# Attention weighting: ScalarE also weighs the last two steps of each batch's last quarter, VectorE's operation there covers two steps

## The chip, the core and the metric

The kernel runs on one core of a Trainium2 chip. The metric is device time in microseconds (us) of one execution, the median of several runs. The engines are TensorE (PE in the profile, PEld for its weight loads), VectorE (DVE), ScalarE (ACT), GpSimd (POOL) and SyncE (SP); each works through its own instructions in order, and they wait for one another by semaphores.

## What is computed

A two-layer graph network over 3125 nodes and 53125 edges (25000 pairs in both directions and one loop a node), all in float32. Each layer adds a message-passing step, a mixer and a mixture of experts to the nodes' features. The change concerns only the message passing of the first layer, attention over the edges into a node, with 8 heads of 32 columns:

```
q = (x @ Wq + bq).reshape(n, H, C)
k = (x @ Wk + bk).reshape(n, H, C)
v = (x @ Wv + bv).reshape(n, H, C)
alpha = jnp.einsum('ehc,ehc->eh', q[dst], k[src]) / jnp.sqrt(jnp.float32(C))
amax = jax.ops.segment_max(alpha, dst, num_segments=n)
ex = jnp.exp(alpha - amax[dst])
denom = jax.ops.segment_sum(ex, dst, num_segments=n)
attn = ex / denom[dst]
msg = (v[src] * attn[:, :, None]).reshape(-1, H * C)
out = jax.ops.segment_sum(msg, dst, num_segments=n)
```

The kernel multiplies v[src] by ex (this is the weighting), sums the weighted rows and ex itself by node, and divides once a node later.

## The kernel before

The edges are sorted by their target and cut into 440 steps of up to 128 edges that belong to one block of 128 nodes. Four steps are a half (`hh`; the prediction calls its place in a batch half 0 to 3, and the title a quarter), two steps are a duo or pair (`p`), and 16 steps are a batch (`j`): 27 full batches and one of 8 steps. `at_kv` holds 32 steps, each with a K part (256 columns), a V part (256) and 8 columns for ex.

What each engine does in `attention`, lines 887 to 1260, in its own fixed order:

- GpSimd (line 949) gathers K and V rows of each step's edges, one indirect DMA a step. A gather waits until TensorE has summed the step 32 before it.
- TensorE `fetch(dd)` (line 1041): for a pair of steps, spreads q from nodes to edges, 6 matmuls (the profile shows two fetches in a row as one row of 12). `attend(j, x)` (lines 1052 and 1066): for pair x of a batch, one matmul that clears and then the matmuls that sum the weighted V rows and ex by node. Their stationary operand is the edge one-hot.
- ScalarE `edge_hot(hh)` (lines 988 and 993): builds the edge one-hot of one half, four Abs and one Relu of the four together. Line 1014 is the exponential of each half, four in a batch. `weigh` (line 1003) multiplies V by ex for half 2: for each of 4 steps and 8 heads one Copy of 32 columns with a scale.
- VectorE `multiply` (1138) multiplies K by q, `reduce` (1147) sums over a head, `weight` (1156) multiplies V by ex for halves 0, 1 and 3, 1024 columns an operation, `add` (1167) adds a pair's sums to `acc`. Between them stands the maximum by segments: scans (1231, 1232, 1239, 1240, 1248, 1249) over scores that TensorE has transposed (line 1088).

Scores and maximum of batch j are made while batch j - 1 is attended. In TensorE's order a cycle is: `fetch` of two pairs, pair 0, a fetch, pairs 1 to 3, a fetch, pairs 4 and 5, a fetch (`at + 8`), pairs 6 and 7, two fetches (`at + 9`, `at + 10`), the transpose of the new scores. In VectorE's: the weighting of half 0 and 1, of half 3 (behind `add` of pair 3), `add` of pairs 4 and 5, the last reductions, `add` of 6 and 7, and then the scans, at whose end line 1255 makes what ScalarE's exponential of the next batch reads.

Pairs 4 and 5 belong to half 2, pairs 6 and 7 to half 3. A pair's matmuls wait for the edge one-hot of their half (`built`) and for its weighting (`weighted`, counted by VectorE's operations, or `weighed`, by ScalarE's steps). Here "one-hot 2" is that of half 2 of the batch being attended, made by `edge_hot(4 * j + 2)`.

Of the kernel before, what the change touches and what calls it, by code (L numbers as in the profile page):

```python
# [14 lines left out]
P = 128  # L15
N = 3125
D = 256
# [14 lines left out]
H1 = 8  # L32
# [67 lines left out]
def wide(ap, shape):  # L100
    return ap.to_broadcast(shape)
# [779 lines left out]
Q4 = U // 2  # L881
# [5 lines left out]
def attention(nc, k, e, q_parts, kv_tab, acc):  # L887
# [3 lines left out]
    HD = D // H1  # L891
# [5 lines left out]
    with Scope(nc) as s:  # L897
        kv = s.sb("at_kv", [P, RING * Q4, 2 * D + H1])
# [34 lines left out]
        weighed = s.sem("at_weighed")  # L933

        def slot(hh):
            return slice(hh % RING * Q4, hh % RING * Q4 + Q4)

        def halves_of(j):
            return list(range(4 * j, min(4 * j + 4, halves))) if 0 <= j < batches else []

        with nc.Block(no_gpsimd_drain=True) as block:
            @block.gpsimd
            def _(pool):
                for t in range(T1):
                    if t >= RING * Q4:
                        pool.wait_ge(summed, t - RING * Q4 + 1)
                    if t >= AHEAD + 2:
                        pool.wait_ge(multiplied, (t - AHEAD) // 2)
                    nc.gpsimd.indirect_dma_start(  # L949
                        out=kv[:, t % (RING * Q4), 0:2 * D], out_offset=None, in_=kv_tab,  # L950
                        in_offset=bass.IndirectOffsetOnAxis(ap=e.src[:, t:t + 1], axis=0)).then_inc(got[t // Q4 % RING], 16)
# [25 lines left out]
            @block.scalar  # L977
            def _(act):
                a = nc.scalar.activation
                made = [0]  # L980

                def edge_hot(hh):
                    if hh >= halves:
                        return
                    if hh:
                        act.wait_ge(built, hh)
                    for u in range(Q4):
                        a(away_e[:, u, :], k.count_row[:, 0:P], ACT.Abs, bias=e.rel[:, hh * Q4 + u:hh * Q4 + u + 1], scale=-1.0).then_inc(away, 1)
                    made[0] += Q4
                    act.wait_ge(away, made[0])  # L990
                    if hh >= NEDGE:
                        act.wait_ge(summed, (hh - NEDGE + 1) * Q4)
                    a(hot_e[:, hh % NEDGE], away_e[:, :, :], ACT.Relu, bias=k.ones[:, 0:1], scale=-1.0).then_inc(built, 1)  # L993

                def weigh(j, us):
                    hh = 4 * j + 2
                    if hh >= halves:
                        return
                    act.wait_ge(exped, hh + 1)
                    for u in us:  # L1000
                        for h in range(H1):
                            row = kv[:, hh % RING * Q4 + u, D + h * HD:D + (h + 1) * HD]
                            ins = a(row, row, ACT.Copy, scale=kv[:, hh % RING * Q4 + u, 2 * D + h:2 * D + h + 1])  # L1003
                        ins.then_inc(weighed, 1)

                edge_hot(0)
                for j in range(batches):
                    if j:
                        act.wait_ge(fell, j)
                        a(fade[:, j % 2:j % 2 + 1], fall[:, j % 2:j % 2 + 1], ACT.Exp, scale=SCALE).then_inc(faded, 1)  # L1010
                    act.wait_ge(diffed, j + 1)
                    for x, hh in enumerate(halves_of(j)):
                        act.wait_ge(got[hh % RING], 16 * Q4 * (hh // RING + 1))
                        a(kv[:, slot(hh), 2 * D:W + D], below[:, x * Q4:(x + 1) * Q4, :], ACT.Exp, scale=SCALE).then_inc(exped, 1)
                    edge_hot(4 * j + 1)
                    weigh(j, (0, 1))
                    weigh(j, (2, 3))
                    edge_hot(4 * j + 2)
                    edge_hot(4 * j + 3)
                    edge_hot(4 * j + 4)  # L1020

            @block.tensor
            def _(pe):
# [21 lines left out]
                def attend(j, *xs):  # L1045
                    for x in xs:
                        p = j * U + x
                        if j < 0 or p >= duos:
                            continue
                        if p >= 2:  # L1050
                            pe.wait_ge(added, p - 1)
                        nc.tensor.matmul(ps_a[p % 2][:, 1, 0:W], nothing[:, 0:P], nothing[:, :], start=True, stop=False, skip_group_check=True)
                        pe.wait_ge(built, p // 2 + 1)
                        if p // 2 % 4 == 2:
                            pe.wait_ge(weighed, Q4 * (p // 8 + 1))
                        else:
                            pe.wait_ge(weighted, p // 8 * 3 + (0, 1, 0, 2)[p // 2 % 4] + 1)
                        for u in range(2):
                            t = 2 * p + u
                            if u == 0:  # L1060
                                to = ps_a[p % 2][:, 0, 0:W]
                            else:
                                r = nc.s_assert_within(where[p // Q4][U + p % Q4], 0, 1,
                                                       skip_runtime_bounds_check_because="a step's block is its neighbour's or the next one")
                                to = ps_a[p % 2][:, ds(r, 1), 0:W].rearrange("p a w -> p (a w)")
                            nc.tensor.matmul(to, hot_e[:, t // Q4 % NEDGE, t % Q4, :], kv[:, t % (RING * Q4), D:2 * D + H1],  # L1066
                                             start=(u == 0), stop=(u == 1), skip_group_check=True).then_inc(summed, 1)
                        if p % Q4 == Q4 - 1:
                            del where[p // Q4]
                for x in range(4):  # L1070
                    fetch(x)
                for j in range(batches + 1):
                    at, i = U * j, j - 1
                    fetch(at + 4)
                    fetch(at + 5)
                    attend(i, 0)
                    fetch(at + 6)
                    attend(i, 1, 2, 3)
                    fetch(at + 7)
                    attend(i, 4, 5)  # L1080
                    fetch(at + 8)
                    attend(i, 6, 7)
# [22 lines left out]
            def _(dve):  # L1105
                v = nc.vector
# [43 lines left out]
                def weight(A, x):  # L1150
                    if x >= len(A):
                        return
                    hh = A[x]
                    dve.wait_ge(exped, hh + 1)
                    rows = kv[:, slot(hh), D:2 * D].rearrange("p u (h d) -> p u h d", d=HD)
                    v.tensor_tensor(rows, rows, wide(kv[:, slot(hh), 2 * D:2 * D + H1].unsqueeze(3), [P, Q4, H1, HD]),
                                    ALU.mult).then_inc(weighted, 1)

                def add(j, x):
# [33 lines left out]
                for j in range(batches + 1):  # L1193
                    S, A, i, at = halves_of(j), halves_of(j - 1), j - 1, U * j
                    last = j == batches
                    h, x = j % 2, score[:, j % 2]
                    load(2 * i)
                    multiply(at + 3)
                    rescale(i)
                    weight(A, 0)  # L1200
                    reduce(S, 0)
                    weight(A, 1)
                    if 1 <= i < batches:
                        dve.wait_ge(rescaled, i)
# [7 lines left out]
                    add(i, 3)  # L1212
                    multiply(at + 5)
                    weight(A, 3)
                    add(i, 4)
                    reduce(S, 2)
# [2141 lines left out]
```

## Time and profile before

| | us |
|---|---|
| median of 3 runs | 3025.67 |
| the runs | 3021.57 to 3026.47 |
| the profiled execution | 3023.47 |
| its span | 3021.7 |
| VectorE busy in the span | 2035.0 (67%) |
| TensorE busy | 2281.1 (75%) |
| GpSimd busy | 1641.5 (54%) |
| ScalarE busy | 1375.9 (46%) |

The profiled execution is one run of the program with every instruction recorded; all durations and places below come from it. Its span starts at 0 with the first instruction. The attention lies between about 284 and 1003 us. "Granted clock" is the share of TensorE's full clock (1.00 is 2.4 GHz, 0.50 is 1.2 GHz). A matmul's end is modelled.

### The profile page before, as it was taken

The page shows a single profiled execution, that of the slowest core. Times are in us where ns is not written, and L with a number is a line of the kernel's source. Part 1 is how long each engine was busy: PE and PEld are TensorE (multiplying, and loading weights), DVE is VectorE, ACT ScalarE, POOL GpSimd, SP SyncE. Part 2 cuts the span into 40 slices and gives each one's busy share as a digit, 9 for nine tenths or more (in the row PEclk, how much of TensorE's full clock was granted, in tenths as well). Part 3 has the DMA queues.
Part 4 walks back from the last instruction along what each step waited for, and adds up shares of the span by engine and source line. Part 5 has one row for each costly group of instructions (what it writes and reads, how often), then busy time and mean ns, then how long its engine had stood idle before and what let it go on. Part 6 is the DMA issues. An engine that isn't in the chain of part 4 may idle for free. (4 is left out here: it accounts for less than half of the span.)

```text
span 3021.7 us, 41600 instructions
## 1 busy us (share of the span) xinstructions
PE 2281.1 (75%) x11076; PEld 1512.9 (50%) x11076; DVE 2035.0 (67%) x4208; ACT 1375.9 (46%) x4369; POOL 1641.5 (54%) x1754
## 2 busy tenths in 40 slices
PE   3997777777777656699965578777778788888785
PEld 2554455555555455556623223222337677777664
DVE  4564899999999888701075699999984722222586
ACT  0221566666666244321242588888972122222232
POOL 1544766666664204567776677777752077777200
PEclk8998788888888855599976799999989689989898
DMA  3212766666664022233232233333321211111004
GB/s 105 54 41 80 217 192 197 195 193 193 195 193 140 1 58 73 58 88 94 87 85 62 82 105 105 103 104 105 105 63 16 61 37 36 32 37 37 17 1 182
DMA packets 165629, 289.12 MB, mean 96 GB/s; under 512 B 55933, under 2 KB 99970, under 8 KB 165407
## 3 DMA queue, kind: packets, MB, share of 16 engines
q0 software_dynamic: 79344, 187.14, 22.8%
q1 hardware_dynamic: 73906, 80.60, 8.6%
q10 hardware_dynamic: 12156, 18.72, 1.7%
q8 instruction: 102, 1.67, 0.2%
q14 instruction: 121, 0.98, 0.1%
HBM read 250.08 MB, written 36.25 MB: 95 GB/s over the span
## 5 line engine op out<-in xcount | busy, mean ns | idle before, releaser
L949 POOL DMA_INDIRECT at_kv<-kv_tab,e_src x440 | 431.9, 981 | 265.5 <-PE at_a L1066 152.4
L2358 PE MATMUL cv_ps<-cv_msg,cv_hot 128*128 128x512 f32 x880 | 431.1, 632 | 145.3 <-DVE acc L2413 126.5
L2345 POOL DMA_INDIRECT cv_x<-x_tab,e_src x440 | 423.7, 963 | 147.7 <-issue 98.8
L2794 POOL DMA_INDIRECT gs_h<-h_tab,fc_q x312 | 295.1, 946 | 184.9 <-issue 93.6
L2358 PEld LDWEIGHTS cv_ps<-cv_msg,cv_hot 128*128 128x128 f32 x880 | 162.0, 198 | 414.1 <-ACT cv_msg L2371 252.6
L2009 POOL DMA_INDIRECT pairs<-gating_pair,gating_place x281 | 275.9, 982 | 149.0 <-issue 66.5
L2371 ACT ACTIVATE cv_msg<-cv_x,factors 128x64 f32<-128x64 f32 x1320 | 356.5, 333 | 0.0
L2413 DVE TENSOR_TENSOR acc<-acc,cv_ps 128x256 f32 x880 | 306.9, 412 | 6.5 <-PE cv_ps L2358 3.8
L2369 ACT ACTIVATE cv_msg<-cv_x,factors 128x256 f32<-128x256 f32 x440 | 217.8, 495 | 122.6 <-DMA cv_x<-x_tab,e_src 122.6
L1066 PE MATMUL at_a<-at_kv,at_hot_e 128*128 128x264 f32 x880 | 252.9, 416 | 13.9 <-ACT at_hot_e L993 9.9
L1041 PE MATMUL at_q<-q_parts,at_hot_n 128*128 x1320 | 228.2, 329 | 42.5 <-DVE at_hot_n L1128 21.1
L2751 ACT ACTIVATE gs_x_hid<-gs_x_h,x_b 128x128 f32<-128x128 f32 x320 | 91.5, 369 | 303.9 <-PE gs_x_h L2718 303.9
L2728 PE MATMUL gs_x_y<-x_w,gs_x_hid 128*128 128x256 f32 x640 | 171.6, 419 | 51.6 <-DVE gs_y L2758 51.5
L1041 PEld LDWEIGHTS at_q<-q_parts,at_hot_n 128*128 128x128 bf16 x1320 | 147.3, 113 | 112.7 <-issue 61.2
L1066 PEld LDWEIGHTS at_a<-at_kv,at_hot_e 128*128 128x128 f32 x880 | 163.7, 207 | 47.3 <-ACT at_hot_e L993 19.0
L1003 ACT ACTIVATE at_kv<-at_kv 128x32 f32<-128x32 f32 x864 | 185.6, 306 | 0.0
L1167 DVE TENSOR_TENSOR acc<-acc,at_a 128x528 f32 x220 | 154.0, 700 | 39.5 <-PE at_a L1066 31.9
L2871 DVE TENSOR_REDUCE gs_as_dst<-gs_d 128x32 f32<-128x96 f32 x39 | 10.1, 258 | 250.7 <-DMA gs_h<-h_tab,fc_q 250.7
L2728 PEld LDWEIGHTS gs_x_y<-x_w,gs_x_hid 128*128 128x128 f32 x640 | 128.7, 210 | 73.7 <-issue 46.9
L2718 PE MATMUL gs_x_h<-xnT,x_w 128*128 128x128 f32 x1280 | 161.0, 283 | 0.0
L2718 PEld LDWEIGHTS gs_x_h<-xnT,x_w 128*128 128x128 f32 x1280 | 157.9, 199 | 2.7
L1138 DVE TENSOR_TENSOR at_kv<-at_kv,at_q 128x512 f32<-128x512 f32 x220 | 147.2, 680 | 15.9 <-DVE at_ends L1240 6.1
(546 smaller groups left out, 4437.9 us busy)
## 6 DMA issues: line engine op xcount, KB each, us to landing
x_space<-in_L_ffn_w SPq DMA_DIRECT2D x16, 1024.0 KB, 7.0
at_rel_row<-e_rel_rows SPq DMA_DIRECT2D x55, 256.0 KB, 4.5
experts_out<-gs_y ACTq DMA_DIRECT2D x20, 512.0 KB, 2.7
x_y<-experts_out SPq DMA_DIRECT2D x20, 512.0 KB, 6.9
at_kv<-kv_tab,e_src POOLq DMA_INDIRECT x440, 3.7
cv_x<-x_tab,e_src POOLq DMA_INDIRECT x440, 2.8
kv_tab<-p_qkv SPq DMA_DIRECT2D x25, 256.0 KB, 2.0
gs_h<-h_tab,fc_q POOLq DMA_INDIRECT x312, 2.4
```

The lines of the kernel that those rows point to most:

```text
L949: nc.gpsimd.indirect_dma_start(out=kv[:, t % (RING * Q4), 0:2 * D], out_offset=None, in_=kv_tab, in_offset=bass.IndirectOffsetOnAxis(ap=e. ...
L1041: ins = nc.tensor.matmul(ps_q[dd % 3][:, u, :], hot_n[:, t // Q4 % NHOT, t % Q4 * P:(t % Q4 + 1) * P], q_parts[:, ds(b, 1), n, :].rearrang ...
L1066: nc.tensor.matmul(to, hot_e[:, t // Q4 % NEDGE, t % Q4, :], kv[:, t % (RING * Q4), D:2 * D + H1], start=(u == 0), stop=(u == 1), skip_gro ...
L2009: nc.gpsimd.indirect_dma_start(out=pairs, out_offset=bass.IndirectOffsetOnAxis(ap=place_i[:, c:c + 1], axis=0), in_=pair[:, c, :], in_offs ...
L2345: nc.gpsimd.indirect_dma_start(out=xg[:, i % RT, u, :], out_offset=None, in_=x_tab, in_offset=bass.IndirectOffsetOnAxis(ap=e.src[:, t:t + ...
L2358: nc.tensor.matmul(ps[u % R][:, :], hot[:, i % 2, u, :], msg[:, i % 2, u, :], start=True, stop=True).then_inc(summed, 1)
L2369: nc.scalar.activation(msg[:, h, u, 0:D], xg[:, i % RT, u, :], ACT.Copy, scale=factor[:, t:t + 1, 0])
L2371: ins = nc.scalar.activation(msg[:, h, u, D + m * M:D + (m + 1) * M], xg[:, i % RT, u, 0:M], ACT.Copy, scale=factor[:, t:t + 1, 1 + m])
L2413: v.tensor_tensor(row, row, ps[u % R][:, n * D:(n + 1) * D], ALU.add).then_inc(added, 1)
L2718: ins = self.nc.tensor.matmul(self.ps_h[e % 2][:, f * P:(f + 1) * P], self.x1.w1[:, e, c, f * P:(f + 1) * P], self.xnT[:, c, b * P:(b + 1) ...
L2728: ins = self.nc.tensor.matmul(self.ps_y[e % 2][:, 0:D], self.hid[:, e % 2, f, :], self.x1.w2[:, e, f, :], start=(f == 0), stop=(f == FX // ...
L2794: nc.gpsimd.indirect_dma_start(out=hg[:, i % RT, u, :], out_offset=None, in_=h_tab, in_offset=bass.IndirectOffsetOnAxis(ap=e.src[:, i * U ...
```

## The change

`weigh` gets the half as an argument. Besides half 2 of each batch, ScalarE weighs the last two steps of half 3, 16 more Copy instructions, placed behind one-hot 2 and ahead of one-hot 3. VectorE's operation for half 3 covers only its first two steps. Pair 6 still waits for VectorE's count and pair 7 now for ScalarE's, which grows by 6 steps a batch where it grew by 4.

```diff
-                def weigh(j, us):
-                    hh = 4 * j + 2
+                def weigh(j, x, us):
+                    hh = 4 * j + x
...
                     edge_hot(4 * j + 1)
-                    weigh(j, (0, 1))
-                    weigh(j, (2, 3))
+                    weigh(j, 2, (0, 1))
+                    weigh(j, 2, (2, 3))
                     edge_hot(4 * j + 2)
+                    weigh(j, 3, (2, 3))
                     edge_hot(4 * j + 3)
                     edge_hot(4 * j + 4)
...
                         if p // 2 % 4 == 2:
-                            pe.wait_ge(weighed, Q4 * (p // 8 + 1))
+                            pe.wait_ge(weighed, 6 * (p // 8) + Q4)
+                        elif p % 8 == 7:
+                            pe.wait_ge(weighed, 6 * (p // 8) + 6)
                         else:
                             pe.wait_ge(weighted, p // 8 * 3 + (0, 1, 0, 2)[p // 2 % 4] + 1)
...
-                    rows = kv[:, slot(hh), D:2 * D].rearrange("p u (h d) -> p u h d", d=HD)
-                    v.tensor_tensor(rows, rows, wide(kv[:, slot(hh), 2 * D:2 * D + H1].unsqueeze(3), [P, Q4, H1, HD]),
+                    n = Q4 if x < 3 else 2
+                    mine = slice(slot(hh).start, slot(hh).start + n)
+                    rows = kv[:, mine, D:2 * D].rearrange("p u (h d) -> p u h d", d=HD)
+                    v.tensor_tensor(rows, rows, wide(kv[:, mine, 2 * D:2 * D + H1].unsqueeze(3), [P, n, H1, HD]),
                                     ALU.mult).then_inc(weighted, 1)
```

ScalarE's order in one batch before, from the exponentials (L1014) on; L988 and L993 are an edge one-hot, L1003 the weighting:

```order
L1014 ACTIVATE at_kv<-at_below 128x4x8 x4
L988 ACTIVATE at_away_e<-count_row,e_rel 128x128 x4
L993 ACTIVATE at_hot_e<-at_away_e,ones 128x512
L1003 ACTIVATE at_kv<-at_kv 128x32 x32
L988 ACTIVATE at_away_e<-count_row,e_rel 128x128 x4
L993 ACTIVATE at_hot_e<-at_away_e,ones 128x512
L988 ACTIVATE at_away_e<-count_row,e_rel 128x128 x4
L993 ACTIVATE at_hot_e<-at_away_e,ones 128x512
L988 ACTIVATE at_away_e<-count_row,e_rel 128x128 x4
L993 ACTIVATE at_hot_e<-at_away_e,ones 128x512
```

And now, at the same place:

```order
L1014 ACTIVATE at_kv<-at_below 128x4x8 x4
L988 ACTIVATE at_away_e<-count_row,e_rel 128x128 x4
L993 ACTIVATE at_hot_e<-at_away_e,ones 128x512
L1003 ACTIVATE at_kv<-at_kv 128x32 x32
L988 ACTIVATE at_away_e<-count_row,e_rel 128x128 x4
L993 ACTIVATE at_hot_e<-at_away_e,ones 128x512
L1003 ACTIVATE at_kv<-at_kv 128x32 x16
L988 ACTIVATE at_away_e<-count_row,e_rel 128x128 x4
L993 ACTIVATE at_hot_e<-at_away_e,ones 128x512
L988 ACTIVATE at_away_e<-count_row,e_rel 128x128 x4
L993 ACTIVATE at_hot_e<-at_away_e,ones 128x512
```

The one-hots of half 3 and of the next batch's half 0 moved behind 16 copies. (Line numbers of ScalarE's rows stay; VectorE's weighting is line 1156 before and 1161 after.)

VectorE's order around the weighting of half 3 before:

```order
330 L1138 TENSOR_TENSOR at_kv<-at_kv,at_q 128x2x256
331 L1128 TENSOR_SCALAR at_hot_n<-at_rel_row,count_col 128x512
332 L1156 TENSOR_TENSOR at_kv<-at_kv 128x4x256
333 L1167 ISA
334 L1167 TENSOR_TENSOR acc<-acc,at_a 128x528
```

And now:

```order
330 L1141 TENSOR_TENSOR at_kv<-at_kv,at_q 128x2x256
331 L1131 TENSOR_SCALAR at_hot_n<-at_rel_row,count_col 128x512
332 L1161 TENSOR_TENSOR at_kv<-at_kv 128x2x256
333 L1172 ISA
334 L1172 TENSOR_TENSOR acc<-acc,at_a 128x528
```

Nothing moved here; the operation covers 2 steps of 256 columns instead of 4. TensorE's order is the same before and after.

## Rows read from the trace of the kernel before

**Rows 1.** The page's first line:

```profile
span 3021.7 us, 41600 instructions
```

**Rows 2.** Windows: length, busy time (x instructions) of PE, PEld, DVE, ACT, POOL; clock; DMA:

```profile
300.00:1000.00 700.00, 521.78 (x2601) 360.84 (x2601) 636.65 (x1227) 416.72 (x1546) 419.29 (x427) 0.82 0.63 186
```

**Rows 3.** Waits from 300 to 1000 us: total, times, longest:

```profile
PEld at_a L1066 <- ACT at_hot_e L993: 19.0, 18, 2.5
...
DVE at_runs L1231 <- PE at_t L1088: 0.9, 1, 0.9
```

**Rows 4.** Groups by line, 300 to 1000 us: busy us, mean ns of one:

```profile
L1003 ACT ACTIVATE at_kv<-at_kv 128x32 f32<-128x32 f32 x864 | 185.6, 306 | 0.0
...
L1138 DVE TENSOR_TENSOR at_kv<-at_kv,at_q 128x512 f32<-128x512 f32 x216 | 144.6, 680 | 11.7 <-DVE at_ends L1240 6.1 <-DMA at_kv<-kv_tab,e_src 2.8 <-issue 0.9
...
L1156 DVE TENSOR_TENSOR at_kv<-at_kv 128x1024 f32<-128x1024 f32 x83 | 100.9, 1217 | 0.0
```

**Rows 5.** Timeline of ScalarE: start, length of the merged row [idle before it]:

```profile
317.14 0.59 ACT L1014 ACTIVATE at_kv<-at_below 128x32 f32<-128x32 f32 x4 [24.87 <-DVE at_below L1255]
...
643.53 0.59 ACT L1014 ACTIVATE at_kv<-at_below 128x32 f32<-128x32 f32 x4 [0.59 <-DVE at_below L1255]
...
645.32 0.72 ACT L993 ACTIVATE at_hot_e<-at_away_e,ones 128x512 f32<-128x512 f32 x1
645.95 6.87 ACT L1003 ACTIVATE at_kv<-at_kv 128x32 f32<-128x32 f32 x32
652.73 1.26 ACT L988 ACTIVATE at_away_e<-count_row,e_rel 128x128 f32<-128x128 f32 x4
654.02 0.72 ACT L993 ACTIVATE at_hot_e<-at_away_e,ones 128x512 f32<-128x512 f32 x1
...
656.09 0.72 ACT L993 ACTIVATE at_hot_e<-at_away_e,ones 128x512 f32<-128x512 f32 x1
...
668.57 0.59 ACT L1014 ACTIVATE at_kv<-at_below 128x32 f32<-128x32 f32 x4 [0.59 <-DVE at_below L1255]
...
970.29 0.59 ACT L1014 ACTIVATE at_kv<-at_below 128x32 f32<-128x32 f32 x4 [0.59 <-DVE at_below L1255]
```

**Rows 6.** Timeline of TensorE, pair 4 to the transpose of the scores:

```profile
654.79 1.16 PE L1066 MATMUL at_a<-at_kv,at_hot_e 128*128 128x264 f32 x4 [0.25 <-ACT at_hot_e L993]
...
655.90 1.05 PE L1066 MATMUL at_a<-at_kv,at_hot_e 128*128 128x264 f32 x4
...
657.56 1.05 PE L1066 MATMUL at_a<-at_kv,at_hot_e 128*128 128x264 f32 x4
...
658.72 1.10 PE L1066 MATMUL at_a<-at_kv,at_hot_e 128*128 128x264 f32 x4
659.66 1.49 PE L1041 MATMUL at_q<-q_parts,at_hot_n 128*128 x12
661.57 0.33 PE L1088 MATMUL at_t<-ident,at_score 128*128 128x128 f32 x1 [0.42 <-DVE at_score L1225]
```

**Rows 7.** Timeline of VectorE, the add of pair 7 and the first scan:

```profile
662.34 0.70 DVE L1167 TENSOR_TENSOR acc<-acc,at_a 128x528 f32 x1 [0.21 <-DVE acc L1167]
662.96 0.41 DVE L1231 TENSOR_TENSOR_SCAN at_runs<-at_flags,at_t 128x128 f32<-128x128 f32 x1
```

**Rows 8.** Timeline in the last full batch: its pair 4, its first scan:

```profile
981.55 1.16 PE L1066 MATMUL at_a<-at_kv,at_hot_e 128*128 128x264 f32 x4 [2.17 <-ACT at_hot_e L993]
...
986.96 0.41 DVE L1231 TENSOR_TENSOR_SCAN at_runs<-at_flags,at_t 128x128 f32<-128x128 f32 x1
```

**Rows 9.** Timeline of TensorE early in the next cycle, fetches and pair 0:

```profile
669.80 2.74 PE L1041 MATMUL at_q<-q_parts,at_hot_n 128*128 x12 [0.52 <-DVE at_hot_n L1128]
...
672.55 1.97 PE L1066 MATMUL at_a<-at_kv,at_hot_e 128*128 128x264 f32 x4
```

**Rows 10.** Windows as in rows 2: an early stretch of a cycle, and an empty one:

```profile
669.80:674.50 4.70, 4.70 (x18) 3.35 (x19) 3.95 (x5) 4.67 (x20) 0.59 (x1) 0.50 0.52 172
979.40:981.50 2.10, 0.00 (x0) 0.00 (x0) 1.84 (x2) 2.06 (x6) 0.00 (x0) 1.00 0.00 0
```

## The prediction

> **What bounds the kernel now.** The profiled execution has a span of 3021.7 us [rows 1], 3023.47 us with what lies around it; the median of the three timed runs is 3025.67 us. Only the attention is touched, so I read that stage alone, engine by engine: from 300 to 1000 us VectorE is busy 636.65 of 700 us, TensorE 521.78, ScalarE 416.72, GpSimd 419.29 [rows 2]. By the shares VectorE is the bound and ScalarE has 40% of the stage free, which is what the change spends. Shares are means over a cycle, though, so next come the waits and then one cycle.
>
> The waits: VectorE almost never waits for the transposed scores (once, 0.9 us), while the weight loads of line 1066 already wait 18 times for ScalarE's edge one-hot [rows 3]. So ScalarE, idle as it is on the average, is late at one place of the cycle.
>
> The cycle: 26 of the 28 batches take 25.12 us on the mean, (970.29 - 317.14)/26 between the starts of line 1014 [rows 5]. I count from such a start; in the sample batch it is 643.53, and the next is 668.57. In this cycle batch j's steps are attended. ScalarE's copies (half 2) run from 645.95 to 652.73, one-hot 2 is ready at 654.02 + 0.72 = 654.74 (+11.21), one-hot 3 at 656.09 + 0.72 = 656.81 (+13.28) [rows 5]. TensorE starts pair 4 at 654.79, 0.05 behind one-hot 2, having waited 0.25; pair 6 at 657.56 (+14.03), pair 7 at 658.72, the two fetches at 659.66, the transpose of the scores at 661.57 [rows 6]. VectorE adds pair 7 at 662.34 and starts the first scan at 662.96 [rows 7]. Over the 26 batches that scan stands on the mean 19.57 us behind the cycle's start, and 5.55 us before the next one (26 pairs of a row of line 1014 and one of line 1231, of which 643.53, 662.96 and 668.57 stand in the rows [rows 5, 7]). A cycle is thus: from the start to the scan, and the serial scans behind it.
>
> **The change part by part.** *VectorE's part removed.* Line 1156 takes 1.217 us for 1024 elements; no row has the same form with 512, the nearest is line 1138, 512 elements, 0.680 us [rows 4]. Half of 1.217 would be 0.61. I take 0.68, the row of the same size: 0.54 us saved in each of 27 batches, 14.5 us if VectorE alone set the cycle.
>
> *ScalarE's part added.* Two steps of eight heads are 16 copies in each of 27 batches, 432 in all. One lasts 306 ns, but 32 of them begin and end within 645.95 to 652.73, so 0.212 us each [rows 4, 5]; 16 take 3.39 us, 91.5 us over the stage. Their amount fits into ScalarE's idle time, but not their place: they stand between one-hots 2 and 3. Copies begin 0.63 us behind the start of the one-hot before them (645.32 to 645.95), and the next one-hot is ready 2.01 us behind their end (652.73 to 654.74) [rows 5]. So one-hot 3 is ready at 654.02 + 0.63 + 3.39 + 2.01 = 660.05, +16.52 instead of +13.28. Its user, pair 6, stands at +14.03 now: 0.75 us of slack against 3.24 us of delay.
>
> *What queues behind that wait.* TensorE works in order. Behind pair 6 stand pair 7, the two fetches and the transpose. Pair 6 starts at +16.57. Pair 7 is 1.11 behind it (654.79 to 655.90), the fetches 0.94 behind that (658.72 to 659.66), and their 12 matmuls last 1.49 us at full clock; the next matmul may start 0.05 before a group's modelled end (654.79 + 1.16 against 655.90) [rows 6]. The transpose then starts at 16.57 + 1.11 + 0.94 + 1.49 - 0.05 = +20.06, lasts 0.33, and the scan follows 0.05 later (the gap seen from one-hot to matmul): +20.44.
>
> *VectorE at that time.* It reaches add 6 half a microsecond earlier than now, waits for pair 6, and can start add 7 when pair 7 is done, 16.57 + 1.11 + 1.05 = +18.73, about +18.8. The scan is 0.62 behind add 7 (662.34 to 662.96) [rows 7], so at +19.4 it would be free; it waits one more microsecond for the transpose. The 0.54 us saved stand before these waits and are lost in them whole. What is late next is the transpose, a wait that is hardly there now.
>
> *The new waits themselves.* TensorE's wait of pair 7 on the copies costs nothing: they end at 654.02 + 0.63 + 3.39 = +14.5, before one-hot 3. One-hot 4, pushed to about +18.6, is needed by the first pair of the next cycle, beyond +25. GpSimd's gathers are released by pairs 6 and 7 about 2.5 us later; it is busy 419.29 of 700 us [rows 2], a share that a longer cycle lowers further, so I take it as hidden.
>
> *The sum.* In 26 batches the scan moves from +19.57 to +20.44, and the 5.55 us behind it stay: 26 x 0.87 = 22.6 us. The last full batch has no fetches and no next scores, so it gets the delay nearly undiluted: pair 6 at 970.29 + 16.57 = 986.86, pair 7 at 987.97, done at 989.02, add 7 at 989.07, scan at 989.69 instead of 986.96 [rows 8]: 2.7 us. Together 25.3 us, which is 3048.8 on the profiled execution's 3023.47 and **3051 us** on the median. In this case alone, with the start of the transpose uncertain by 0.25 us a batch, the time lies between 3043 and 3058.
>
> The Trainium skill, "ScalarE: Activation LUTs", section "Rules for kernel authors", sends multiplications to VectorE and not to ScalarE. Here that rule would also have the change lose, by engine time: 3.39 us of ScalarE bought with 0.54 us of VectorE. The sum does not rest on it.
>
> **The rivals.** *The clock falls in the new hole.* TensorE now has nothing between about +14.2 and +16.57. At the lower clock (0.5 granted, 1.2 GHz, from 669.80 to 674.50 [rows 10]) 12 fetch matmuls take 2.74 us and a pair 1.97, against 1.49 and 1.05 [rows 9, 6]. For two pairs and the fetches this is 0.92 + 0.92 + 1.25 = 3.1 us at most, all on the path. That stretch lies behind the sparse one around the transpose, so a cycle does lose the clock where it is sparse. Against it speak two rows: before the last full batch's pair 4 TensorE waited 2.17 us, and the grant stayed at 1.00 (2.4 GHz) through the empty stretch, the pair lasting 1.16 us [rows 8, 10]. If it falls in a third of the batches, 9 x 2.7 = 24 us more: 3075. In all of them: 3124. [...]
>
> *The delay is hidden.* If TensorE had the transpose out before VectorE wants it, the scan would stand at +19.4, 0.17 us earlier than now: 26 x -0.17 + 2.7 = -2 us, 3024, no change. It decides whether 12 matmuls lie between pair 7 and the transpose; by the program they do.
>
> *VectorE stays the bound (the change does what the shares promise).* Then 27 x 0.54 = 14.5 us are gained: 3011. This needs one-hot 3 ready by +14.1, that is 16 copies in 0.8 us instead of 3.39. The rows of the 864 copies leave no room for it [rows 4].
>
> **How the numbers follow.** Forecast (one-hot 3 late, clock held) 0.64: 3051. Clock falls in part of the batches 0.24: 3075 and beyond. Hidden 0.07: 3024. VectorE's gain 0.05: 3011. The range of 8 in 10 takes the forecast's own and the clock's up to a third of the batches: 3040 to 3076. About 0.2% (6 us) is what a measurement can tell: faster 0.05, same 0.07, slower 0.88.
>
> **What would show it.** In the profile after: TensorE's wait for the edge one-hot, 19.0 us of weight loads now, grows by some 27 x 2.3 = 60 us; a wait of VectorE's scan for the transpose appears, about 1 us in each of 26 batches; the starts of the exponentials stand about 26.0 apart; the 2-step operation lasts 0.68 us; ScalarE's copies number 1296. Wrong: pair 6 starting before +16, the scan before +20, the 2-step operation with no wait behind it, or matmuls of pairs 6 and 7 near 2 us (the clock).

## The result and the profile after

| | us |
|---|---|
| before, median of 6 runs | 3025.35 (3020.24 to 3026.47) |
| changed, median of 6 runs | 3086.26 (3083.67 to 3088.01) |
| ratio, with its 95% interval | 1.0205 (1.0192 to 1.0218) |
| the changed kernel's profiled span | 3081.3 |

The change costs 61 us, where 25 were forecast and 51 was the end of the range. The direction and the place were right, the size was not. Busy time does not explain it, as the page's first part and the window over the attention (with columns as in [rows 2]) show:

```profile
span 3081.3 us, 42031 instructions
...
PE 2317.4 (75%) x11075; PEld 1546.4 (50%) x11076; DVE 2023.6 (66%) x4208; ACT 1464.4 (48%) x4801; POOL 1629.8 (53%) x1754
```

```profile
300.00:1052.00 752.00, 548.06 (x2578) 383.75 (x2578) 618.82 (x1217) 503.09 (x1971) 406.01 (x426) 0.79 0.59 173
```

In the whole span VectorE works 11 us less, ScalarE 88 us and TensorE 36 us more, all of them with time to spare, and the stage is 62 us longer: from the first batch's exponentials to the last one's it was 991.59 - 317.14 = 674.45 us and is 1052.52 - 315.90 = 736.62. The waits from 300 to 1060 us, with columns as in [rows 3]:

```profile
DVE acc L1172 <- PE at_a L1069: 90.8, 136, 3.8
PEld at_a L1069 <- ACT at_hot_e L993: 78.8, 32, 3.2
...
DVE at_runs L1236 <- PE at_t L1091: 22.4, 27, 1.6
```

The weight loads' wait for the one-hot went from 19.0 to 78.8 us, and a wait of the first scan for the transpose appeared, 22.4 us against 0.9 [rows 3]. One cycle shows how. ScalarE, in the cycle that starts at 644.83:

```profile
644.83 0.59 ACT L1014 ACTIVATE at_kv<-at_below 128x32 f32<-128x32 f32 x4 [0.59 <-DVE at_below L1260]
...
655.33 0.72 ACT L993 ACTIVATE at_hot_e<-at_away_e,ones 128x512 f32<-128x512 f32 x1
655.96 3.49 ACT L1003 ACTIVATE at_kv<-at_kv 128x32 f32<-128x32 f32 x16
...
660.64 0.72 ACT L993 ACTIVATE at_hot_e<-at_away_e,ones 128x512 f32<-128x512 f32 x1
```

One-hot 3 is ready at 661.36, +16.53; the prediction had +16.52. TensorE, from pair 6 to the transpose, which answers to [rows 6]:

```profile
661.42 2.13 PE L1069 MATMUL at_a<-at_kv,at_hot_e 128*128 128x264 f32 x4 [2.39 <-ACT at_hot_e L993]
...
663.56 1.56 PE L1069 MATMUL at_a<-at_kv,at_hot_e 128*128 128x264 f32 x4
664.96 1.47 PE L1042 MATMUL at_q<-q_parts,at_hot_n 128*128 x12
666.27 0.27 PE L1091 MATMUL at_t<-ident,at_score 128*128 128x128 f32 x1
```

Pair 6 starts at +16.59 and lasts 2.13 us, pair 7 1.56; in the cycle below that kept its clock they take 1.16 and 1.05. The windows say why: the grant falls from 1.00 to 0.50 (2.4 to 1.2 GHz) at the end of the empty stretch.

```profile
658.80:661.30 2.50, 0.23 (x3) 0.00 (x0) 2.50 (x7) 2.47 (x9) 1.89 (x2) 0.97 0.70 213
661.60:664.60 3.00, 3.00 (x8) 2.20 (x9) 1.88 (x3) 1.80 (x5) 2.39 (x3) 0.50 0.76 221
```

By windows of 0.4 us over the stage, this happens between +16.3 and +17.9 in 26 of the 27 cycles: from the last tenths of the hole to 1.3 us behind its end, when pair 6 or 7 is running. Pair 6's wait is 1.95 to 2.39 us in the first 26 cycles and 2.96 in the last. The one cycle that held its clock, through a wait of 2.15 us, is a control within the profile; its pair 6, fetches and transpose:

```profile
743.34 1.16 PE L1069 MATMUL at_a<-at_kv,at_hot_e 128*128 128x264 f32 x4 [2.15 <-ACT at_hot_e L993]
...
744.44 1.05 PE L1069 MATMUL at_a<-at_kv,at_hot_e 128*128 128x264 f32 x4
745.33 1.47 PE L1042 MATMUL at_q<-q_parts,at_hot_n 128*128 x12
746.64 0.27 PE L1091 MATMUL at_t<-ident,at_score 128*128 128x128 f32 x1
```

It took 25.76 us, the others of the first 26 27.40 us on the mean. VectorE in the cycle from 644.83 waits for pair 6, for pair 7 and for the transpose, one after the other:

```profile
663.69 0.70 DVE L1172 TENSOR_TENSOR acc<-acc,at_a 128x528 f32 x1 [0.88 <-PE at_a L1069]
665.27 0.70 DVE L1172 TENSOR_TENSOR acc<-acc,at_a 128x528 f32 x1 [0.87 <-PE at_a L1069]
666.65 0.42 DVE L1236 TENSOR_TENSOR_SCAN at_runs<-at_flags,at_t 128x128 f32<-128x128 f32 x1 [0.68 <-PE at_t L1091]
```

### The profile page after: what moved, and what is told of

Read it like the earlier page. It is cut to its first block and busy times, and to the rows that moved or that the text cites. A ratio compares the mean times of both kernels' runs of the same rounds, so it can differ in the third digit from the quotient of the medians.

```text
span 3081.3 us, 42031 instructions
## 1 busy us (share of the span) xinstructions
PE 2317.4 (75%) x11075; PEld 1546.4 (50%) x11076; DVE 2023.6 (66%) x4208; ACT 1464.4 (48%) x4801; POOL 1629.8 (53%) x1754
## 5 line engine op out<-in xcount | busy, mean ns | idle before, releaser
L949 POOL DMA_INDIRECT at_kv<-kv_tab,e_src x440 | 419.4, 953 | 331.4 <-PE at_a L1069 191.9
L1069 PE MATMUL at_a<-at_kv,at_hot_e 128*128 128x264 f32 x880 | 297.6, 475 | 69.9 <-ACT at_hot_e L993 66.0
L1003 ACT ACTIVATE at_kv<-at_kv 128x32 f32<-128x32 f32 x1296 | 279.7, 306 | 0.0
L1069 PEld LDWEIGHTS at_a<-at_kv,at_hot_e 128*128 128x128 f32 x880 | 187.8, 236 | 121.5 <-ACT at_hot_e L993 78.8
L1141 DVE TENSOR_TENSOR at_kv<-at_kv,at_q 128x512 f32<-128x512 f32 x220 | 147.4, 681 | 12.7 <-DVE at_ends L1245 6.2
```

The source lines that it names most:

```text
L949: nc.gpsimd.indirect_dma_start(out=kv[:, t % (RING * Q4), 0:2 * D], out_offset=None, in_=kv_tab, in_offset=bass.IndirectOffsetOnAxis(ap=e. ...
```

## The experiments

All were timed in turn with the kernel before on the same chip; its medians there were 3026.6, 3023.3 and 3024.5 us for the three groups of runs. Where two medians differ by a few microseconds I also give the stage, from the first batch's exponentials to the last one's, in the two profiles: two profiles of one kernel agree there to 0.2 us (653.81 and 653.62, the run with one-hots built ahead and its repetition), while what lies behind the stage takes 2027 to 2035 us in the 13 profiles, without a tie to the edit.

### Is it the clock, or the late one-hot itself?

**The hole filled.** In the changed kernel's `attend`, behind the clearing matmul:

```diff
+                        for _ in range(18 if x == 6 else 0):
+                            nc.tensor.matmul(ps_a[p % 2][:, 1, 0:W], nothing[:, 0:P], nothing[:, :], start=True, stop=False, skip_group_check=True)
```

> The changed kernel with 18 more clearing matmuls (zeros, bfloat16, the same as the one that is there) on TensorE ahead of pair 6's wait, in the hole of 2.4 us. It computes the same. Theory (the clock falls in the hole): with the hole filled the granted clock stays at 1.00 until behind the transpose, pairs 6 and 7 last 1.16 and 1.05 us again, the cycle is 25.8 us as in the one batch that held its clock, and the time is 3086.3 - 26 x 1.6 = about 3045 us, although TensorE does more. Rival (ScalarE's copies into at_kv slow TensorE's or VectorE's access to the same memory, and the clock only goes along with it): pairs stay near 2 us and the time at 3083 or above.

3041.1 us, 1.0049 of before (1.0031 to 1.0066). TensorE in the same place now:

```profile
667.79 2.19 PE L1055 MATMUL at_a<-at_nothing 128*128 128x264 bf16 x18
670.22 1.16 PE L1071 MATMUL at_a<-at_kv,at_hot_e 128*128 128x264 f32 x4 [0.24 <-ACT at_hot_e L993]
```

No cycle loses its clock there, the mean of the first 26 is 25.78 us, and 45 of the 61 us are gone, by 486 matmuls more on zeros and nothing else. What stays, 14.5 us on the medians and 694.31 - 674.45 = 19.9 us between the exponentials of the two profiles, is the delay alone. The copies' access to the memory is not the cause of these 45 us: they are all still there.

**The delay alone.** In the kernel before, between one-hots 2 and 3:

```diff
                     edge_hot(4 * j + 2)
...
+                        for n in range(16):
+                            ins = a(idle[:, n, :], k.count_row[:, 0:HD], ACT.Copy, scale=k.ones[:, 0:1]).then_inc(idled, 1)
                     edge_hot(4 * j + 3)
```

> The kernel before, VectorE's operations as they were, with 16 copies of 32 columns into a scratch tile between one-hots 2 and 3: the delay alone, with nothing weighed by it. Theory (one-hot 3's delay and the hole are all that matters, VectorE's 0.54 us saved are lost in its waits): the time is that of the changed kernel, 3083 to 3090 us. Rival (the copies' access to at_kv): no such access here, so cycles near 25.8 to 26.0 and 3045 us. If VectorE's saving had counted after all, 3086 + 14.5 = 3101.

3088.0 us, 1.0200 (1.0183 to 1.0217): the whole loss, although ScalarE weighs no more than before and VectorE's operations have their full size. Pair 6 of one cycle:

```profile
663.13 2.13 PE L1074 MATMUL at_a<-at_kv,at_hot_e 128*128 128x264 f32 x4 [2.53 <-ACT at_hot_e L995]
```

Its one-hot 3 is 0.14 us later than the changed kernel's. The clock falls in 25 of the 27 cycles; the two that keep it do so through waits of 2.34 and 2.53 us. So what VectorE saves is worth next to nothing here, not 14.5 us.

### How long may the hole be?

**Nine matmuls instead of 18**, which leaves pair 6 a wait of 0.9 to 1.4 us (1.9 in the last full batch).

> As the run with 18 clearing matmuls ahead of pair 6's wait, with 9: the hole on TensorE shrinks from 2.4 to about 1.4 us and is not closed. It computes the same. Theory (the length of the hole decides whether the clock falls in it): 1.4 us is less than the 2.17 us that one pair of before waited through at full clock, so the clock holds in nearly all batches: 3041 to 3048 us. Rival (any hole in this place drops it): 3080 us or more; a mixture of cycles of 25.8 and 27.3 us would put it between.

3043.0 us, 1.0066 (1.0049 to 1.0083), as with the hole closed. The clock falls in none of the 27. One of them:

```profile
669.24 1.16 PE L1071 MATMUL at_a<-at_kv,at_hot_e 128*128 128x264 f32 x4 [1.24 <-ACT at_hot_e L993]
```

**Four**, which leaves 1.4 to 1.9 us (2.5 in the last full batch).

> The changed kernel with 4 clearing matmuls more ahead of pair 6's wait: a hole of about 1.9 us, between the 1.4 us that held the clock in the run with 9 and the 2.4 us of the changed kernel that lost it in 26 of 27 batches. It computes the same. If the hole's length decides with an edge below 1.9 us: cycles of 27.3 us and 3080 or more. If the edge lies above: 25.8 and 3043. If it depends on where in the cycle the hole falls as well: both kinds of cycle in one run, between 3043 and 3086.

3056.4 us, 1.0110 (1.0089 to 1.0130): both kinds of cycle in one run. In the profile 5 of 27 lose the clock, the other cycles take 25.8. Pairs 6 and 7 of a cycle that lost it and of one that held it, the hole alike:

```profile
544.05 1.19 PE L1071 MATMUL at_a<-at_kv,at_hot_e 128*128 128x264 f32 x4 [1.93 <-ACT at_hot_e L993]
545.25 1.97 PE L1071 MATMUL at_a<-at_kv,at_hot_e 128*128 128x264 f32 x4
...
597.24 1.16 PE L1071 MATMUL at_a<-at_kv,at_hot_e 128*128 128x264 f32 x4 [1.93 <-ACT at_hot_e L993]
598.35 1.05 PE L1071 MATMUL at_a<-at_kv,at_hot_e 128*128 128x264 f32 x4
```

So length is not all. In the five that fell the hole was 1.9 us and the clock had risen at +3.9 to +4.3 of the same cycle; in those that held it rose at +4.4 or later, up to +7.9. All five fell at +17.6 to +17.9, 1.0 to 1.3 us behind the hole's end. The hole of 1.4 us never lost it here, that of 1.9 us sometimes, that of 2 us and more nearly always (51 of the 54 cycles of the changed kernel and of the run with the delay alone). That the place of the hole against the clock's earlier rise counts as well is what the five and the 22 suggest; no run moved the one without the other.

### Smaller versions of the edit

**One-hot 3 ahead of the copies.**

```diff
                     edge_hot(4 * j + 2)
-                    weigh(j, 3, (2, 3))
                     edge_hot(4 * j + 3)
+                    weigh(j, 3, (2, 3))
                     edge_hot(4 * j + 4)
```

> The changed kernel with one-hot 3 ahead of the 16 added copies and not behind them. It computes the same. One-hot 3 is ready at +13.3 as in the kernel before, pair 6 starts on time at +14.0, and pair 7 waits for the copies until about +16.8, a hole of 1.6 us between the pairs. Theory: pair 7 stands 0.9 us earlier than in the changed kernel, the transpose at +19.0, the scan at +19.4, about where it is in the kernel before, and the clock holds in the shorter hole: 3020 to 3030 us. If the clock falls here too, in all batches: about 3065. Rival (the order of the two doesn't matter, the copies' 3.39 us do): 3080 and above.

3025.5 us, 1.0006 (0.9996 to 1.0015): no loss, and no gain. Pair 7 now waits, 1.0 to 1.5 us, and the clock holds in each of the first 26 cycles. In the cycle that starts at 641.93:

```profile
658.75 1.13 PE L1069 MATMUL at_a<-at_kv,at_hot_e 128*128 128x264 f32 x4 [1.46 <-ACT at_kv L1003]
659.72 1.47 PE L1042 MATMUL at_q<-q_parts,at_hot_n 128*128 x12
661.03 0.27 PE L1091 MATMUL at_t<-ident,at_score 128*128 128x128 f32 x1
```

Two lines in another order take back all 61 us. The same instructions run.

**One step instead of two** (8 copies; VectorE's operation over three steps).

> The changed kernel with half of the edit: ScalarE weighs only the last step of half 3 (8 copies, 1.7 us), VectorE's operation covers three steps (768 elements, about 0.95 us). It computes the same. Theory: one-hot 3 is ready at about +14.9, pair 6 waits 0.7 us, the clock holds, the transpose could start at +18.3 and the scan is VectorE's: it waits for pair 7, done at about +17.1, less than now. So the cycle keeps its length or loses up to 0.27 us: 3018 to 3027 us. Rival (each copy between the one-hots costs its time): half of the loss, about 3055.

3023.5 us, 1.0000 (0.9990 to 1.0010). One-hot 3 is ready at +14.84. Pair 6 waits 0.4 to 0.7 us and keeps its full clock, as in this cycle:

```profile
657.68 1.16 PE L1070 MATMUL at_a<-at_kv,at_hot_e 128*128 128x264 f32 x4 [0.44 <-ACT at_hot_e L993]
```

The transpose stands at +18.2, 1.7 us earlier than in the cycle of the changed kernel that held its clock, and VectorE does not wait for it. The loss is not proportional to the copies: half of them cost nothing.

### What is VectorE's half microsecond worth?

**VectorE's part alone**, in the kernel before: its operation for half 3 covers two steps and nobody weighs the other two.

```diff
+                    n = Q4 if x < 3 else 2
+                    mine = slice(slot(hh).start, slot(hh).start + n)
```

> The kernel before with VectorE's operation for half 3 over two steps and nothing in its place: the last two steps of each full batch's half 3 stay unweighted. ScalarE's and TensorE's instructions are those of before. It prices VectorE's 0.54 us a batch by themselves. Theory (VectorE sets the cycle in the stretch from that operation to the scans once one-hot 3 is on time): 3026 - 14.5 = about 3012 us. Rival (VectorE's time there is slack, and the cycle hangs on pair 4's wait for one-hot 2 at +11.2 and TensorE behind it): no change, 3020 to 3027.

3022.8 us, 1.0006 (0.9996 to 1.0015): nothing; the stage is 674.45 - 673.21 = 1.2 us shorter. Here my theory fell, and the rival with pair 4 stands. VectorE before, in the cycle that starts at 643.53:

```profile
654.84 1.20 DVE L1156 TENSOR_TENSOR at_kv<-at_kv 128x1024 f32<-128x1024 f32 x1
656.10 0.70 DVE L1167 TENSOR_TENSOR acc<-acc,at_a 128x528 f32 x1
```

And in this run, in the cycle that starts at 643.32:

```profile
654.62 0.67 DVE L1158 TENSOR_TENSOR at_kv<-at_kv 128x512 f32<-128x512 f32 x1
655.89 0.70 DVE L1169 TENSOR_TENSOR acc<-acc,at_a 128x528 f32 x1 [0.59 <-PE at_a L1066]
...
662.93 0.41 DVE L1233 TENSOR_TENSOR_SCAN at_runs<-at_flags,at_t 128x128 f32<-128x128 f32 x1
```

The operation is 0.53 us shorter, and the next one, the add of pair 4, waits 0.59 us: it starts at +12.57 in both. Pair 4 starts only when ScalarE's one-hot 2 is ready, at +11.2, change or no change. So it is in 16 of the first 26 cycles; in the other ten pair 4 starts later, at +11.3 to +11.9, behind TensorE's own earlier work. The add of pair 4 waits for TensorE in all 26, and did in 10 before. VectorE is busy 91% of the stage [rows 2] and not what this stretch hangs on.

### ScalarE's order mended

**The one-hots ahead of time**, in the kernel before: those of halves 1 and 2 are built at the end of the cycle before, where ScalarE waits some 9 us.

```diff
                 edge_hot(0)
+                edge_hot(1)
+                edge_hot(2)
...
-                    edge_hot(4 * j + 1)
                     weigh(j, (0, 1))
                     weigh(j, (2, 3))
-                    edge_hot(4 * j + 2)
                     edge_hot(4 * j + 3)
                     edge_hot(4 * j + 4)
+                    edge_hot(4 * j + 5)
+                    edge_hot(4 * j + 6)
```

> The kernel before with the same earlier one-hots and nothing else: what the new order gives alone. Theory: pair 4's waits for one-hot 2 (19.0 us in all, 0.25 to 0.8 us a batch) go, most of it hidden behind VectorE: 3018 to 3026 us. The difference to the changed kernel in the same order is VectorE's 0.54 us in 27 batches, 14.5 us.

3010.0 us, 0.9952 (0.9936 to 0.9967). The gain, 16.5 us on the medians and 674.45 - 664.14 = 10.3 us in the stage, is more than I had expected at most: pair 4's wait was not hidden behind VectorE, the cycle hung on it. Pair 4 now never waits for one-hot 2 in the first 26 cycles, and its add never for pair 4. (The one-hot of half 1 moved too; what each of the two gives was not tried.)

**The same order with the change in it**, `weigh(j, 3, (2, 3))` behind `weigh(j, 2, ...)`.

> The changed kernel with ScalarE's one-hots built ahead: one-hots 1 and 2 of the next batch are built at the end of a cycle, where ScalarE is idle, and behind the exponentials come the weighting of half 2, that of half 3 and only then one-hot 3. It computes the same. Theory (place, not amount, was wrong): one-hot 3 is ready near +12.9, pair 6 doesn't wait, VectorE is the bound and its 0.54 us show: 3011 us, down to 3005 where pair 4's wait goes too. Rival (432 more copies cost by themselves): above 3025.

3006.9 us, 0.9927 (0.9910 to 0.9944). ScalarE does all 48 copies in a row, and one-hot 3 is ready 12.7 us behind the start:

```profile
634.61 0.59 ACT L1016 ACTIVATE at_kv<-at_below 128x32 f32<-128x32 f32 x4 [0.59 <-DVE at_below L1262]
635.11 10.28 ACT L1003 ACTIVATE at_kv<-at_kv 128x32 f32<-128x32 f32 x48
...
646.59 0.72 ACT L993 ACTIVATE at_hot_e<-at_away_e,ones 128x512 f32<-128x512 f32 x1
```

On the medians the change is worth 3 us in this order, not 14.5, and the two intervals overlap. The stage says more: 664.14 - 653.81 = 10.3 us shorter, 0.39 a cycle. Not all of that is VectorE's operation. The clock rises as late as +7 in 4 of the cycles here and in 7 there, and such a cycle takes 25.4 to 25.9 us, the others at most 24.8. In cycles where it rises alike, at +4.1 or at +7.1, the change gives 0.1 to 0.2 us. The add of pair 4 waits 0.2 to 0.5 us for the pair again in 22 of 26. How the 10.3 us divide stays open.

**Once more, beside the next one.**

> The changed kernel with one-hots built ahead once more, beside the run that keeps the clock up, on the same chip: 3003 to 3010 us.

3003.0 us, 0.9930 (0.9911 to 0.9951); the stage is 653.62 us.

**The clock kept up between cycles.** As above, with clearing matmuls (on zeros) in TensorE's idle stretches around the scans:

```diff
+                        if j:
+                            pe.wait_ge(added, U * j)
+                        for _ in range(8 if j else 0):
+                            nc.tensor.matmul(ps_a[0][:, 1, 0:W], nothing[:, 0:P], nothing[:, :], start=True, stop=False, skip_group_check=True)
                         pe.wait_ge(cornered, j + 1)
```

with 4 more ahead of the wait for `linked` and 6 behind `fetch(at + 11)`.

> The changed kernel with one-hots built ahead and, besides, clearing matmuls on TensorE in its idle stretches around the scans (8 behind the transpose once pair 7 is added, 4 ahead of the wait for the scans of the ends, 6 ahead of the last transpose), to keep the clock up to the start of the next cycle. It computes the same. Theory (cycles of that kernel are 24.0 us where the clock rises by +4.4 and 25.4 to 25.7 where it rises at +7.2): all cycles near 24.0 or below, 3006.9 - 26 x 0.3 = 2999 us. Rival (the extra matmuls stand ahead of the chain of scans and lengthen it): 3007 to 3020.

2995.1 us, 0.9900 (0.9877 to 0.9922), the fastest version: 8 us less than the run beside it on the medians, 653.62 - 647.47 = 6.2 us in the stage. The windows over the attention of the kernel without and with these matmuls:

```profile
300.00:970.00 670.00, 503.34 (x2589) 352.44 (x2589) 618.06 (x1219) 507.40 (x1965) 414.35 (x428) 0.83 0.65 194
```

```profile
300.00:965.00 665.00, 538.57 (x3075) 377.76 (x3075) 615.74 (x1220) 507.39 (x1965) 416.40 (x428) 0.92 0.66 196
```

The mean grant goes from 0.83 to 0.92 and the first 26 cycles from 24.37 to 24.13 us. Where the clock never fell (three cycles in a row) they take 24.02, 23.68 and 23.68; where it still rises late, at +7.1 and +7.3, 25.3 and 25.4.

## Why the prediction was right and wrong

- *ScalarE has the time but not the place.* Right, to 0.01 us: one-hot 3 at +16.53, pair 6 at +16.6. The run with the two lines exchanged shows that the place is what costs: the same copies, none of the loss. The run with half of them shows that even in this place a delay costs nothing when it leaves pair 6 a wait of at most 0.7 us, as in its first 26 cycles.
- *The transpose waits behind pair 7 and two fetches, and VectorE for it.* Right as a chain. Its size at full clock was a little too large: the scan stands at +20.27 where the clock holds, not +20.44, so the term of 0.87 us a batch measures 25.76 - 25.12 = 0.64, and 26 of them are 16.6 us, not 22.6. The last full batch adds 24.13 - 21.30 = 2.8 us (2.7 in the sum). From pair 7 to the transpose pass 2.20 us (744.44 to 746.64) where the sum had 0.94 + 1.49 - 0.05 = 2.38. Forecast 25.3, measured 19.9 between the profiles with the hole filled.
- *The clock holds.* This is the step that failed. The forecast let TensorE pass the new hole before pair 6 at full clock; the fall was only a rival, at 0.24, and in a third of the batches for the end of the range. It happened in 26 of 27. Of the 62.2 us between the profiles 42.3 are this. The price of one fall was wrong the other way: the sums for a third and for all batches used 2.7 us, without a working for it, and it measured 1.6 us for the mean cycle (27.40 - 25.76), since the clock comes back between +19.7 and +21.3, before or during the fetches. So all batches at once came to 3086 and not 3124. What misled me is a single row, the wait of 2.17 us at full clock [rows 8]. It stands ahead of another pair and at another place of the cycle. That hole is there in the changed kernel too, ahead of pair 4 of the last full batch, and the clock held in it again, as in every other profile that has it (the hole filled, nine matmuls, the delay alone, one step):

```profile
1037.98 1.16 PE L1069 MATMUL at_a<-at_kv,at_hot_e 128*128 128x264 f32 x4 [2.17 <-ACT at_hot_e L993]
```

The row was true, and said nothing of a hole ahead of pair 6. What sets the two places apart, no run tried.
- *VectorE's 0.54 us are lost in the later waits.* The conclusion was right and the reason wrong, so here the forecast was lucky. They are lost at once, in the wait for pair 4. So the rival "VectorE stays the bound, 3011 us" had a false price: taken alone, without a single copy added, the edit gives nothing. I had the rows for it, pair 4's wait of 0.25 us and one-hot 2 at +11.21 [rows 5, 6], and read them as a warning about ScalarE only. VectorE's operation ended at 656.04 and pair 4 at 655.95, so the two chains were balanced, and shortening one could not help.
- *The waits' own figures.* Forecast 60 us more for the one-hot, measured 59.8; forecast about 1 us a batch of the scan for the transpose, measured 22.4/27 = 0.8, and 16.5/27 = 0.6 with the hole filled; VectorE's waits for gathers stayed at 2.9 us in the stage (2.8 before), as forecast; 0.68 us for the operation of 512 elements, measured 0.70 (0.68 in the run of VectorE's part alone). Of the signs I had named for the clock, pairs near 2 us, the profile after shows one of 1.8 to 2.1 us in each of 26 cycles.

## What to carry to other kernels

An engine's idle share says that work fits, not where: ask of every piece that is moved onto an engine what stands behind it in that engine's order and who waits for it, and put the piece behind what is awaited. Before shortening an operation, look whether the next one on that engine waits for another engine at that moment; a wait of a few tenths behind it is enough to swallow the gain. And price a new hole on TensorE twice, at full and at half clock: a row in which the clock held through a hole at another place of the cycle is no bound.

## What was not expected of the hardware

- The clock fell in or just behind a hole of 1.95 to 2.4 us of TensorE in a stretch otherwise dense, in 25 of the first 26 cycles; with holes of at most 1.4 us at the same place in none of the first 26, and with holes of at most 1.9 us in 5 of them. Longer ones held it at times: 2.15 us in the changed kernel, 2.34 and 2.53 in the run with the delay alone. Zeros keep it up: the filling matmuls have nothing but zeros for operands.
- The falls can keep step with the cycle. In the changed kernel nine cycles in a row (480.95 to 726.75) took 27.30 to 27.33 us, each with its fall at +16.3 to +16.4, while the first 25 cycles of before take 24.9 to 25.6 and their falls wander between +20.0 and +23.3. Whether the length of the cycle that a fall brings makes the next fall likelier was not tried separately; it would be one reason why a chance that looked small came up nearly every time.
- Matmuls added to TensorE made the kernel faster in two places, by 45 us in the hole and by 8 us on the medians around the scans.
